# Row maxima of the attention scores: four products in row groups of 32 rows, run two slots ahead, and their negated row laid down by a transfer

## The reference

```python
# layer 0 has a mask, layer 1 a gate on the values; B, S, NK = 8, 100, 1444
x = x + tanh(g_xattn[0]) * xattn0(layernorm(x), ctx, ctx, Wq, bq, Wk, bk, Wv, bv, Wo, bo, mask)
x = x + tanh(g_ffn[0])   * moe0(layernorm(x), ...)        # 64 experts, 8 chosen, one shared
x = x + tanh(g_xattn[1]) * xattn1(layernorm(x), ctx, ctx, energy, ...)
x = x + tanh(g_ffn[1])   * moe1(layernorm(x), ...)        # 8 experts, 2 chosen

# inside an attention
scores = einsum('bhqd,bhkd->bhqk', q, k) / sqrt(8)        # masked in layer 0
attn   = softmax(scores, axis=-1)                         # the maximum of each row is subtracted
out    = einsum('bhqk,bhkd->bhqd', attn, v) @ Wo + bo     # layer 1: attn * sigmoid gate of the key
```

## Time and profile before

| | us |
|---|---|
| median of 3 runs | 1072.9 (1072.05 to 1076.41) |
| the profiled execution's own time | 1076.31 |
| its span, first to last instruction | 1074.5 |
| first maxima read in layer 0, in layer 1 (from the span's start) | 35.73, 611.16 |
| PE busy, share of the span | 936.5, 87% |
| DVE busy | 760.5, 71% |
| ACT busy | 588.5, 55% |
| POOL busy | 351.4, 33% |

### The profile page before, as it was taken

How to read it: one execution, slowest core, us unless ns; L and a number is a source line. 1 busy time by engine, 2 the same in 40 slices (tenths; PEclk the granted TensorE clock), 3 DMA queues, 4 the chain that set the end, 5 groups by cost and what they waited for, 6 DMA issues and landing times.

```text
span 1074.5 us, 24455 instructions
## 1 busy us (share of the span) xinstructions
PE 936.5 (87%) x9740; PEld 708.0 (66%) x9740; DVE 760.5 (71%) x1459; ACT 588.5 (55%) x1194; POOL 351.4 (33%) x278
## 2 busy tenths in 40 slices
PE   4589999999999989579998679999999998851996
PEld 2247677777777766468887347677777766541885
DVE  6987777676767764749997897766766765041996
ACT  2125565655565566336665227667667667621664
POOL 5800221303022110037676532243144132001774
PEclk8879999999999999679999789999999998955999
DMA  6630404134040500086652550431341340016661
GB/s 165 117 90 2 112 29 85 47 67 98 16 112 2 114 1 2 1 201 173 167 166 77 115 124 5 109 94 47 85 112 41 73 114 1 2 17 124 164 169 54
DMA packets 48088, 88.52 MB, mean 82 GB/s; under 512 B 21154, under 2 KB 31558, under 8 KB 47974
## 3 DMA queue, kind: packets, MB, share of 16 engines
q1 hardware_dynamic: 47974, 86.96, 34.0%
HBM read 47.24 MB, written 1.75 MB: 46 GB/s over the span
## 4 chain that ended last, share of the span: by engine, by line
PE 60%; DVE 15%; POOL 9%; ACT 6%; issue 5%; DMA 4%; SPq 1%; POOLq 0%; DVEq 0%; ACTq 0%
PE ps L1139 16%; PE po L1159 14%; PE pm L1110 14%; POOL tmpf L768 6%; PE ps L1142 6%; PE pc L1091 3%; PE pc L1078 3%; DVE vaug L530 3%; DVE qsel L521 3%; ACT qsel L928 3%; DMA routing<-vaug 2%; ACT probs L844 2%; POOL qbd L684 2%; DVE mx_part L412 1%; DVE junk L417 1%
## 5 line engine op out<-in xcount | busy, mean ns | idle before, releaser
L844 ACT ACTIVATE probs<-ps 121x400 f32<-121x400 f32 (+1 forms) x768 | 370.1, 505 | 236.7 <-PE ps L1142 145.1
L1139 PE MATMUL ps<-qst,kst 128*121 128x400 f32 (+1 forms) x768 | 306.3, 415 | 20.9 <-ACT probs L844 18.8
L1110 PE MATMUL pm<-khi,qbd 128*100 128x482 f32 (+1 forms) x696 | 247.4, 438 | 26.7 <-DVE mx_part L417 10.0
L412 DVE TENSOR_REDUCE mx_part<-pm 128x2 f32<-128x964 f32 (+1 forms) x160 | 178.5, 1134 | 55.2 <-PE pm L1110 55.0
L1139 PEld LDWEIGHTS ps<-qst,kst 128*121 128x121 f32 (+1 forms) x768 | 139.6, 185 | 104.2 <-ACT probs L844 61.6
L1244 PE MATMUL pm<-qsel,qst 128*128 128x400 f32 x660 | 159.5, 366 | 39.3 <-DVE qsel L521 35.4
L417 DVE CUSTOM_DVE_ANT_0 junk<-pm,negq 100x964 bf16<-100x964 f32 x128 | 148.0, 1160 | 58.4 <-PE pm L1110 58.1
L1159 PE MATMUL po<-probs,vaug 121*32 121x100 f32 x6144 | 173.7, 254 | 1.4 <-ACT probs L844 1.4
L1159 PEld LDWEIGHTS po<-probs,vaug 121*32 121x32 f32 x6144 | 130.8, 110 | 56.6 <-ACT probs L844 30.1
L1110 PEld LDWEIGHTS pm<-khi,qbd 128*100 128x100 f32 (+1 forms) x696 | 122.0, 183 | 65.4 <-DVE mx_part L417 18.8
L1244 PEld LDWEIGHTS pm<-qsel,qst 128*128 128x128 f32 x660 | 123.3, 197 | 58.4 <-DVE qsel L521 57.5
(11 more groups left out here) (176 smaller groups left out, 964.6 us busy)
## 6 DMA issues: line engine op xcount, KB each, us to landing
kst<-khi SPq DMA_DIRECT2D x128, 180.5 KB, 3.9
wb<-routing SPq DMA_DIRECT2D x66, 200.0 KB, 3.6
ctxT<-in_ctxT SPq DMA_DIRECT2D x16, 722.0 KB, 4.3
kst<-klo SPq DMA_DIRECT2D x64, 180.5 KB, 3.9
wts<-in_experts SPq DMA_DIRECT2D x55, 192.0 KB, 3.8
wb<-routing SPq DMA_DIRECT2D x22, 400.0 KB, 4.0
qsel<-qhi SPq DMA_DIRECT2D x16, 100.0 KB, 2.4
routing<-vaug SPq DMA_DIRECT2D x1, 1100.0 KB
```

Source lines behind the costliest of these rows:

```text
L412: nc.vector.tensor_reduce(mx_part[0:rows, i * 3 + c:i * 3 + c + len(items)], bank[:, 0:len(items), :], AX, ALU.max).then_inc(s["max_taken" ...
L844: nc.scalar.activation(probs[t % 2][0:r, g * GQ:(g + 1) * GQ], ps[0:r, n % 2, 0:GQ], ACT.Exp, scale=SCALE).then_inc(s["probs_ready"], 1)
L1110: mm = nc.tensor.matmul(pm[0:rows, n % 2 * 2 + j, 0:MAX_W], qbd[b % 2][:, first:first + rows], khi[b % 2][:, lo:lo + MAX_W], start=True, s ...
L1139: mm = nc.tensor.matmul(ps[0:r, n % 2, 0:GQ], kst[b % 2][:, g, t * KEY_TILE:t * KEY_TILE + r], qst[b % 2][:, g * GQ:(g + 1) * GQ], start=T ...
```

## The change

- A product contracts only the 32 rows of its own group of four heads and is placed on those rows of the array (`tile_position=(32 * g, 0)`). `qbd` shrinks from 1600 to 400 columns: column block j holds head j of each of the four groups.
- Four products make a run, or quad (`max_quad`, L1114 to L1117 after; `quad_max` on DVE). It fills all four banks `pm`, and DVE reads it in two halves of two banks. Layer 1 now has 48 products too. In layer 0 a quad is of kind `MAX_PAIR` (two groups with two chunks each; banks written in the order 0, 2, 1, 3) or `MAX_THIRD` (four groups, the third chunk); in layer 1 always `MAX_CHUNK` (four groups, one chunk, banks 0 to 3).
- A batch has 12 quads, one in each slot, two slots ahead: slots 10 and 11 hold the first two quads of the batch after next (`QUADS_AHEAD`, `ROW_SLOT` = 10). The first two quads of batch 1 run before slot 0 of batch 0. In layer 0 PE makes the quad after score group 1, ahead of `weigh`; in layer 1 after group 2.
- The row of maxima: DVE's L430 writes `rowmax`, PE transposes it in slot 10, ACT negates it into `mrow` [16, 100] (`max_row`, between exponentials 2 and 3 of slot 10), and a transfer on the SP queue lays the 16 rows end to end in row 96 of `qst` (`row`). The DVE writes L438 are gone, and score matmuls contract 97 rows. `scores` of slot 0 waits for the transfer.
- POOL makes `qbd` for two batches at the start, later one batch further ahead.

```diff
+MAX_PAIR, MAX_THIRD, MAX_CHUNK = range(3)
+MAX_QUADS = [[q for j in range(J) for q in ((MAX_PAIR, j, 0), (MAX_PAIR, j, 2), (MAX_THIRD, j, 2))],
+             [(MAX_CHUNK, j, c) for j in range(J) for c in range(3)]]
+QUADS_AHEAD = 2
+ROW_SLOT = QUADS - QUADS_AHEAD
...
-        qbd = [sb(f"qbd{i}", [128, HQ], F32R) for i in range(2)]
+        qbd = [sb(f"qbd{i}", [128, GQ], F32R) for i in range(2)]
...
+                def quad_max(b, k):
+                    n, (kind, j, x) = b * QUADS + k, MAX_QUADS[l][k]
+                    if b >= 1 and k == 0:
+                        dve.wait_ge(s["rowmax_ready"], b)
+                    for i in range(2):
+                        bank = pm[0:S, 2 * i:2 * i + 2, 0:MAX_W]
+                        dve.wait_ge(s["chunk_ready"], 2 * n + i + 1)
...
+                        ins.then_inc(s["max_taken"], 1)
...
-                    for lo, hi, w, off in NEGM_WRITES[l]:
-                        nc.vector.tensor_tensor(qst[b % 2][96:128, lo * rows:lo * rows + (hi - lo) * w]
...
+                def max_row(b):
+                    act.wait_ge(s["maxrow_ready"], b + 1)
+                    if b >= 1:
+                        act.wait_ge(s["mrow_in"][(b - 1) % 2], landed(b - 1, (b - 1) % 2, 2, 16))
+                    nc.scalar.activation(mrow[:], pc[0:H, 0:S], ACT.Identity, scale=-1.0).then_inc(s["mrow_ready"], 1)
...
+                def max_quad(b, k):
...
+                    for i, bank in enumerate((0, 2, 1, 3) if kind == MAX_PAIR else (0, 1, 2, 3)):
+                        g, c = (x + bank // 2, bank % 2) if kind == MAX_PAIR else (bank, x)
+                        lo, rows = MAX_STARTS[c], slice(32 * g, 32 * g + 32)
+                        if n >= 1 and i == 0:
+                            pe.wait_ge(s["max_taken"], 2 * n - 1)
+                        if n >= 1 and bank == 2:
+                            pe.wait_ge(s["max_taken"], 2 * n)
+                        mm = nc.tensor.matmul(pm[0:S, bank, 0:MAX_W], qbd[b % 2][rows, j * S:(j + 1) * S],
+                                              khi[b % 2][rows, lo:lo + MAX_W], start=True, stop=True,
+                                              tile_position=(32 * g, 0))
+                        if bank % 2 == 1:
+                            mm.then_inc(s["chunk_ready"], 1)
...
+                        pe.wait_ge(s["mrow_in"][b % 2], landed(b, b % 2, 2, 16))
...
-                    mm = nc.tensor.matmul(ps[0:r, n % 2, 0:GQ], kst[b % 2][:, g, t * KEY_TILE:t * KEY_TILE + r],
+                    mm = nc.tensor.matmul(ps[0:r, n % 2, 0:GQ], kst[b % 2][0:97, g, t * KEY_TILE:t * KEY_TILE + r],
...
+            def row(l, b):
+                sp.wait_ge(A[l]["mrow_ready"], b + 1)
+                sp.dma_start(qst[b % 2][96:97, :].bitcast(F32),
+                             mrow[:].bitcast(F32)).then_inc(A[l]["mrow_in"][b % 2], 16)
...
+                for b in range(2, B):
+                    stack(l, b, b % 2)
+                    if b + 2 < B:
+                        context(l, b + 2, b % 2)
+                    row(l, b)
```

More of the change, by code:

```diff
@@ L394, in attention @@
             def attention(l):
-                s, units, blocks, rows = A[l], MAX_UNITS[l], MAX_BLOCKS[l], MAX_ROWS[l]
+                s = A[l]
+                parts = mx_part[0:S, :].rearrange("q (g j c) -> q g j c", j=J, c=3)
                 def k_low(b, c):
@@ L486, in attention @@
                                                     tgates[0:S, l:l + 1], xres[:], ALU.mult, ALU.add))
-                slots(-1)
+                for k in range(QUADS):
+                    quad_max(0, k)
+                    if k in FIRST_K_TAKEN:
+                        k_low(1, FIRST_K_TAKEN.index(k))
+                row_max(0)
+                for k in range(QUADS_AHEAD):
+                    quad_max(1, k)
                 slots(0)
@@ L1064, in attention @@
             def attention(l):
-                s, units, rows = A[l], MAX_UNITS[l], MAX_ROWS[l]
+                s = A[l]
                 def k_chunk(b, c):
@@ L1406, in attention @@
                 stack(l, 1, 1)
+                row(l, 0)
                 context(l, 3, 1)
-                for i in range((B - 4) // 2):
-                    for k in range(2):
-                        stack(l, i * 2 + (2 + k), k)
-                        context(l, i * 2 + (4 + k), k)
-                stack(l, B - 2, 0)
-                stack(l, B - 1, 1)
+                row(l, 1)
+                for b in range(2, B):
[3 more added lines that the diff above has]
+                    row(l, b)
             def experts(l):
```

165 lines of the change are left out of this document (68 added, 97 removed).

## The result

The changed kernel took **1091.6 us** (median of 4 runs, 1084.8 to 1099.9) against 1073.3: 1.0165 times the time before, with a 95% interval of 1.0132 to 1.0199. Timed once more with the experiments it took 1090.8 (6 runs, 1083.4 to 1103.1), ratio 1.0148 (1.0106 to 1.0190). It is slower by some 1.5%; the forecast was 1069, no change with a lean to faster, and that lean was wrong. Medians and ranges here hold all runs; the ratios leave out single runs over 1.5% above the fastest of their kernel (one each of the second timing here, e1_warm, e3_order, e9_ahead1 and e14_gate). The spread is a result too: the runs of before lie within 5 us of each other, those of after within 15 to 20.

The account below looks back on a forecast made before the run. PE was taken as the bound, with its chain of scores and exponentials setting the slot floor. Terms -15, 0, +2, +10.8 and -1 in each layer gave -4.2: profiled 1076.3 to 1072.1, forecast median 1069 us, range 1046 to 1102.

Parts of the forecast that it names:

- the first slots, at half clock: First slots of each layer: quads cost less there than units at 1.14 us each, put at -1 us in each layer.
- The quad's price: PE time per quad in the slots: layer 0 0.64 us a pair, 0.44 a third; layer 1 0.64 with both shape changes.
- Rivals 1: Row groups of a quad load one after another, some 0.08 us apart: +33 us, 1102 us; chance 0.19.
- rival 2: Change of shape hidden and pairs stream freely in the slots, quads of 0.35 to 0.40 us: 1045 us; chance 0.22.
- Rival 4: Row groups don't overlap at all, quads of 1.1 to 1.3 us: +100 us, 1165 us; chance 0.03.
- The settled batches: Layer 0: 44.6 us a batch against 46.75, -15 us over seven; layer 1: 38.0 against 38.06, no gain.
- The floor: Slot time without any unit, set by PE's chain of scores and exponentials: 2.98 us in layer 0, 2.64 in layer 1.
- the place of its gap: Units between score groups 0 and 1 stood in a gap of PE's chain; the quad stands on the chain in both layers.
- DVE's sum: Layer 1 batch: 24 halves take 25.9 us against 19.5, DVE busy about 31 of 38 us, so not the bound.
- The row's transfer: First score's wait for the row of maxima: none in layer 0, 0.3 us in layer 1, six batches: +2 us.
- Rival 3: The row of maxima lands about 1.5 us late in every batch: +18 us, 1087 us; chance 0.11.
- Before the first slot: First batch's maxima, two quads ahead of slot 0 and smaller `qbd`: +5.0 us in layer 0, +5.8 in layer 1, together +10.8.

Follow-up runs that it names:

- e1_warm: Changed kernel with small products of zeros on PE during the first batch's maxima, ahead of the slots: 1089.7 us, 1.0116 times the kernel before.
- e3_order: Changed kernel with the first batch's pair quads written in bank order 0, 1, 2, 3: 1081.4 us, 1.0052 times the kernel before.
- e9_ahead1: Changed kernel with one quad instead of two running ahead and the row of maxima laid down in slot 11: 1167.8 us, 1.0837 times the kernel before.
- e14_gate: Changed kernel with the work for layer 1's gates moved behind the slots of batch 6 in layer 0: 1081.4 us, 1.0049 times the kernel before.
- e4_gap: Changed kernel with the quad between score groups 0 and 1 in both layers: 1099.1 us, 1.0214 times the kernel before.
- e7_front: Changed kernel with the quad ahead of score group 0 in both layers: 1070.2 us, 0.9963 times the kernel before.
- e17_after_again: Changed kernel without any edit, timed again with the experiments: 1090.8 us, 1.0148 times the kernel before.

## Why the prediction was wrong

**The step that failed** is the sentence "the first slots, at half clock, pay less for the quads than for units (1.14 us a unit), which I put at -1 in each layer", with its premise "In both attentions the clock is granted in full". I read the clock of the first slots as given, a few microseconds long whatever PE does there. It depended on what the change replaced: +5.0 us in the first slots of layer 0 and +8.4 in batch 0 of layer 1, where -2 stood for both, at a granted clock of 0.50 for 20 and 26 us. (The +2.1 in slot 0 of batch 1 comes behind a stall that was not priced either, see the last point.) The Trainium skill ("TensorE: Matmul & The Clock Gate", section "What's actually happening") says that activity releases the throttle. In the kernel before the trace looks like that; after, it doesn't, if activity is the profile's busy share: 19.76 of 19.76 us at 0.50. Here the measurement decides. What is shown is that the loss stands at half clock and that products of zeros in the slots, or zero rows in the scores, shorten it. Which property of the quads takes the clock away stays open.

**Point by point.**
- *The quad's price* was right: 0.39 and 0.62 us for a third and a pair (forecast 0.44 and 0.64), in layer 1 0.39, and 0.21 more for the score after it (0.60, forecast 0.64). Rivals 1 and 4 fall by these rows, and the four loads of a quad take 0.17 us together (230.46), not spaced by 0.08. (Rows 6 give a spacing nearer to 0.10 for 100 columns, which would have made that rival dearer.) Of rival 2 the 0.39 came true, the free change of shape did not: the score behind the quad still pays, and plain intervals are 3.37 to 3.58 and 3.00 us, not 3.0 and 2.7. Rival 4's 1165 is 1169 by its own sum.
- *The settled batches* were right to 0.5 and 0.8 us (44.10 and 37.20 against 44.6 and 38.0): ACT's negation cost nothing that shows (slot 10 takes 3.39 and 2.99 us, no more than plain ones). That is some 6.5 us in all beyond the forecast in batches 2 to 6 of layer 0 and 1 to 6 of layer 1.
- *The floor* (2.98 and 2.64 us, from a chain with exponentials) was right, *the place of its gap* wrong (e4_gap, e7_front): ahead of group 0, not behind it. This error lost the better version, not the forecast's sum.
- *DVE's sum* compares 25.9 us with "19.5", which is the number of units (21.1 us). It did no harm: DVE is busy 29.7 of 37.2 us in a batch of layer 1, where about 31 stood.
- *The row's transfer* costs one wait of 0.46 us in the profiled run where 2 stood. The fear behind the 2 was in part right: in layer 0 the row always lands in 1.7 us, in layer 1 in 2.1 at the median and once in 3.36, with the context issued 2.2 us ahead of it (3.3 in layer 0). Rival 3 is there now and then: e17_after_again shows one late by 0.87 us. Priced at its wait it is nothing; with the clock behind it, 11 us.
- *Before the first slot*: the first stretch grew by 4.5 (4.0 forecast), the way from the row maxima to the first score by 3.9 (2.7), `qbd` gave 1.5 (1.7); from the last batch of layer 0 to the first weigh of layer 1 +4.7 (4.8). What was missing in layer 0 is again half clock: the first weigh came 1.5 us later after the first score than before, where the -1 stood.
- *Not priced*: DVE's gates' work in batch 0. "The four banks without a second set don't stall PE" was worked out for settled slots alone; slot 11 of batch 0 stands 3.5 us above the settled ones where it stood 1.5 above before.

## What to carry to other kernels

A change that packs or narrows matmuls must be priced at both levels of the clock: look up in the trace where PE is at half clock and what PE does when it comes back, and ask whether the new instructions still bring it back. Busy time didn't tell it here; zero rows that keep the products at full height can be worth more than the rows they save. Look at several profiles before you read the length of such a stretch: the same slots were at half clock for 20 us in one and 29 in another. And put extra PE work where PE waits on the chain (here ahead of the first score of a slot): the same quads made the kernel 1.5% slower in one place and 0.4% faster in another.

## What the hardware showed that was not expected

- PE busy for 19.76 of 19.76 us at a granted clock of 0.50, with scores of 97 rows and quads in groups of 32; back after 7 to 17 us with 128 rows in the scores, after 4 in the kernel before. In the changed kernel's profile the clock, once full, stays full through the same slots (1.00 in batches 2 to 6).
- At full clock, a standstill of 0.87 us was followed by 27.3 us at half clock. The kernel before has no such stretch in its batches 1 to 6.
- Four products in four row groups take 0.39 us where one takes 0.22; two in each of two groups 0.62.
- A transfer of 6.2 KB into one row landed in 1.7 us in every batch of layer 0; in layer 1 in 2.1 at the median, once in 3.36 and, in a second profile of the same kernel, once in 3.78. Both of these stood 2.2 us behind the issue of a transfer of 722 KB, but a row without one ahead also took 2.57; the reason is not shown.
